# Local attention in a decoder on one core: score products of one head on half of the array's rows, softmax over eight heads at a time

## The chip, the cores and the metric

The kernel runs on one core of one Trainium2 chip. The metric is the device time of one execution in microseconds (us). A core has TensorE (PE, which multiplies matrices, and PEld, its loading of the stationary operand), VectorE (DVE), ScalarE (ACT), GpSimd (POOL) and the queues that issue DMAs (SP among them). Each runs its own list of instructions in order; semaphores tie the lists together. TensorE's results go to PSUM, eight banks of 512 fp32 numbers for each of 128 partitions; DVE and ACT read them from there.

## The reference, cut to what matters

A decoder of two blocks (a bidirectional Mamba layer, cross attention, a mixture of experts; then local attention, cross attention, another mixture of experts) on 32 sequences of 128 tokens of width 128, all in fp32. The change touches the local attention alone:

```python
H, KV, HD, WIN = 16, 4, 64, 64            # 16 query heads share 4 key/value heads
q = rmsnorm((x @ wq.T).reshape(B, T, H, HD), q_norm_w)
k = rmsnorm((x @ wk.T).reshape(B, T, KV, HD), k_norm_w)
v = (x @ wv.T).reshape(B, T, KV, HD)      # k and v repeated 4 times, to 16 heads
scores = einsum('bqhd,bkhd->bhqk', q, k) / sqrt(HD)
mask = (i >= j) & (i - j < WIN)
attn = softmax(where(mask, scores, -inf))
y = einsum('bhqk,bkhd->bqhd', attn, v).reshape(B, T, H * HD) @ wo.T
```

## The kernel before, in words

`program` (L2534) runs the six layers one after the other. `window_attention_layer` (L1790) walks the 32 sequences; each sequence has four slots q = 0 to 3, one for each quad of four heads that share a key/value head. All engines walk the same slots (`walk_sequences`, L203), each with its own `slot` function, and the order within a slot is the order of the code. In the slot (b, q) an engine works for several sequences at once: b itself, b + 1 (scores and softmax), b + 2 (transposes of q and k), b + 3 (the projection to q, k and v) and b - 1 (the output).

PE, in the order of its slot (L1877):

- `turn` (L1842): four transposes of the normalized probabilities of quad q of b into the PSUM tile `pt`; waits for POOL's `norm_ready`.
- `scores` of quad q of b + 1 (L1852): a product of the identity with the mask `outside` (bf16, 512 columns) sets the bank, then two fp32 products add the scores of two heads each: the stationary operand is a pair of heads of q (two times 64 rows), the moving one `kT`, which holds the transposed keys twice on the diagonal and zeros beside them, so that a product over 128 rows gives two heads. The two tiles `ps` are one bank each and take turns, so that quad q + 1 can be written while quad q is read.
- In slot 1: a transpose of the normalized input of b + 3, and twelve transposes of q and k of b + 2. In slot 2: the projection to q, k and v of b + 3 (L1897, L1899), then the output projection of b - 1 (L1920).
- `values` of the quad before (L1865): probabilities times values, two heads in each half of the columns.

The trace shows two instructions for each fp32 product, and one for each transpose or bf16 product.

DVE, in slot q: the row sum `den` (L2012) of the quad that comes up for division, the row maximum `top` (L2018) of a quad of fresh scores, the reciprocal of the first (L2025), the subtraction of the second (L2031). Behind these in slot 0: `xh` (L2041), then `qn` and `kn` (L2058, L2061), which wait for r, the reciprocal root of the mean squares of b + 2. In slot 2: a copy of v. In slot 3: the sum of squares (L2047) and the mean square (L2051) of b + 3, and the residual sum.

ACT: the copy of `py` to `cT`, exp (L1949) in place on `pr` two slots after the scores, the copy of the transposed probabilities (L1955), in slot 1 the copies to `qT` and `kT` (L1968, L1973: two instructions of 64 partitions for `kT`), in slot 2 the squares (L1980, L1983).

POOL, in slot q: the division `norm` (L2094), a product of `pr` with the reciprocals; in slot 3, behind the division of quad 0 of the next sequence, the power that gives r (L2104). The division of quad 1 in slot 0 stands behind it.

Of the kernel before, what the change touches and what calls it, by code (L numbers as in the profile page):

```python
# [37 lines left out]
QH = 4  # L38
# [1741 lines left out]
def window_weights(nc, ctx, w):  # L1780
    W = Weights(nc, ctx, "dw_")
    W.wq = W.tile("wq", [128, HL * HDL], w["wq"])
    W.wkv = W.tile("wkv", [128, 2 * KVL * HDL], w["wkv"])
    W.wo = W.tile("wo", [128, HL // 2, D], w["wo"])
    W.outside32 = W.tile("outside32", [128, T], w["outside"])
    W.qnw, W.knw = W.tile("qnw", [128, 1], w["qnw"]), W.tile("knw", [128, 1], w["knw"])
    return W


def window_attention_layer(nc, S, W, ahead):  # L1790
# [12 lines left out]
    with ExitStack() as ctx:  # L1803
        A = Alloc(nc, ctx, "d_")
        outside = A.sb("outside", [128, T], BF16)
        kscale = A.sb("kscale", [128, 1])
# [8 lines left out]
        qT = [A.sb(f"qT{p}", [128, NP, T]) for p in range(2)]  # L1815
        kT = [A.sb(f"kT{p}", [128, KVL, 2, T]) for p in range(2)]
        top, den, rden = ([A.sb(f"{n}{q}", [128, QH]) for q in range(NQ)] for n in ("top", "den", "rden"))
        pr = [A.sb(f"pr{q}", [128, QH, T]) for q in range(NQ)]
        prT = [A.sb(f"prT{q}", [128, QH, T]) for q in range(2)]
        cT = [A.sb(f"cT{p}", [128, NP, T]) for p in range(2)]  # L1820
        ps = [A.ps(f"ps{k}", [128, QH, T]) for k in range(2)]
        pt = A.ps("pt", [128, QH, T])
# [5 lines left out]
            ms_ready r_ready qn_ready kn_ready ve_ready v_ready qkT_mm qT_ready kT_ready s_mm top_ready sub_ready  # L1828
            exp_ready den_ready rden_ready norm_ready pt_mm prT_ready y_mm cT_ready o_mm x_ready stats kT_zero""".split()}
        with nc.Block() as block:  # L1830
# [6 lines left out]
            def _(pe):  # L1837
# [4 lines left out]
                def turn(b, q):  # L1842

                    t = b.quad(q)
                    pe.wait_ge(s["norm_ready"], t + 1)
                    if due(t):
                        pe.wait_ge(s["prT_ready"], t)
                    for i in range(QH):
                        ins = tr(pt[:, i, :], pr[q][:, i, :], S.ident[:, :])
                    ins.then_inc(s["pt_mm"], 1)  # L1850

                def scores(b, q):  # L1852
                    t = b.quad(q)
                    if q == 0:
                        pe.wait_ge(s["qT_ready"], 2 * (b.n + 1))
                        pe.wait_ge(s["kT_ready"], 2 * (b.n + 1))
                    if due(t - 1):
                        pe.wait_ge(s["sub_ready"], t - 1)
                    mm(ps[q % 2][:, :, :], S.ident_bf[:, :], bc(outside[:, :], 1, QH), start=True, stop=False)
                    for k in range(2):  # L1860
                        ins = mm(ps[q % 2][:, 2 * k:2 * k + 2, :], qT[b.p][:, 2 * q + k, :], kT[b.p][:, q, :, :],  # L1861
                                 start=False, stop=k == 1)
                    ins.then_inc(s["s_mm"], 1)

                def values(b, q):  # L1865
                    t = b.quad(q)
                    pe.wait_ge(s["prT_ready"], t + 1)
                    if q == 0:
                        pe.wait_ge(s["v_ready"], b.n + 1)
                    if due(t):  # L1870
                        pe.wait_ge(s["cT_ready"], t)
                    for k in range(2):
                        ins = mm(py[64 * k:64 * k + 64, 0:2 * T], v[b.p][:, q, :], prT[q % 2][:, k:QH:2, :],  # L1873
                                 start=True, stop=True)
                    ins.then_inc(s["y_mm"], 1)

                def slot(b, q):  # L1877
                    if b.real():
                        turn(b, q)
                    nxt = b.plus(1)  # L1880
                    if nxt.real():
                        scores(nxt, q)
                    n = b.plus(3)
# [6 lines left out]
                    if q == 2 and n.real():  # L1890
                        pe.wait_ge(s["xT_ready"], n.n + 1)
                        if due(2 * n.n):
                            pe.wait_ge(s["qT_ready"], 2 * n.n)
                        if due(2 * n.n):
                            pe.wait_ge(s["kT_ready"], 2 * n.n)
                        for k in range(2):
# [32 lines left out]
            def _(act):  # L1929
                A_ = nc.scalar.activation  # L1930
                act.wait_ge(s["kscale"], 2)
                act.wait_ge(s["kT_zero"], 2)

                def slot(b, q):
# [28 lines left out]
                    if q == 1 and m.real():  # L1963
                        if due(NQ * (m.n - 1)):
                            act.wait_ge(s["s_mm"], NQ * (m.n - 1))
# [5 lines left out]
                        for k in range(2):  # L1971
                            half = slice(64 * k, 64 * k + 64)
                            A_(kT[m.p][half, :, k, :], pkv[half, :].rearrange("p (i t) -> p i t", t=T), ACT.Copy,  # L1973
                               scale=kscale[half, 0:1]).then_inc(s["kT_ready"], 1)
                    if q == 2 and n.real():
# [18 lines left out]
            def _(dve):  # L1994
                V = nc.vector
                dve.wait_ge(W.loaded, W.all())
                for p in range(2):
                    V.memset(kT[p][:, :, :, :], 0.0).then_inc(s["kT_zero"], 1)
                V.tensor_copy(outside[:, :], W.outside32[:, :]).then_inc(s["prep"], 1)

# [5 lines left out]
                def slot(b, q):  # L2006
                    d = b if q < 3 else b.plus(1)
                    if d.real():
                        qd = (q + 1) % NQ
                        t = d.quad(qd)  # L2010
                        dve.wait_ge(s["exp_ready"], t + 1)
                        V.tensor_reduce(den[qd][:, :], pr[qd][:, :, :], AX.X, ALU.add).then_inc(s["den_ready"], 1)  # L2012
                    a = b if q < 1 else b.plus(1)
                    if a.real():
                        qa = (q + 3) % NQ
                        t = a.quad(qa)
                        dve.wait_ge(s["s_mm"], t + 1)
                        V.tensor_reduce(top[qa][:, :], ps[qa % 2][:, :, :], AX.X, ALU.max  # L2018
                                        ).then_inc(s["top_ready"], 1)
                    if d.real():  # L2020
                        t = d.quad(qd)
                        dve.wait_ge(s["den_ready"], t + 1)
                        if due(t - 3):
                            dve.wait_ge(s["norm_ready"], t - 3)
                        V.reciprocal(rden[qd][:, :], den[qd][:, :]).then_inc(s["rden_ready"], 1)  # L2025
                    if a.real():
                        t = a.quad(qa)
                        dve.wait_ge(s["top_ready"], t + 1)
                        if due(t - 3):
                            dve.wait_ge(s["pt_mm"], t - 3)  # L2030
                        V.tensor_tensor(pr[qa][:, :, :], ps[qa % 2][:, :, :], bc(top[qa][:, :], 2, T),  # L2031
                                        ALU.subtract).then_inc(s["sub_ready"], 1)
# [50 lines left out]
            def _(pool):  # L2083
# [4 lines left out]
                def slot(b, q):  # L2088
                    d = b if q < 3 else b.plus(1)
                    if d.real():  # L2090
                        qd = (q + 1) % NQ
                        t = d.quad(qd)
# [465 lines left out]
def layout(inputs):  # L2558
# [10 lines left out]
    for p in "fb":  # L2569
# [34 lines left out]
    a.update({"D_wq": f[n + "wq"].T, "D_wkv": np.concatenate([f[n + "wk"], f[n + "wv"]]).T,  # L2604
              "D_wo": f[n + "wo"].T.reshape(HL // 2, 128, D).transpose(1, 0, 2),
              "D_outside": np.where((i >= j) & (i - j < WIN), 0.0, MASKED).astype(np.float32),
              "D_qnw": np.tile(f[n + "q_norm_w"], 2)[:, None], "D_knw": np.tile(f[n + "k_norm_w"], 2)[:, None]})
# [33 lines left out]
```

## Time and profile before

| | |
|---|---|
| timed runs, median of 3 (lowest to highest) | 2488.03 us (2478.44 to 2491.33) |
| the profiled execution | 2469.95 us |
| its span, first to last instruction | 2468.2 us |
| mean granted clock of TensorE | 0.924 |
| busy over the span: PE, DVE, ACT, POOL | 84%, 76%, 58%, 57% |
| the local attention's first and last instruction, about | 1527 and 2045 us |

The page cuts the span into 40 slices of 61.7 us; the local attention fills slices 26 to 33. The timeline view lists instructions of an engine in order of time, neighbours of one kind merged; the duration that it gives for several is from the first start to the last end, so the time that they hold the engine is better read from start to start. In square brackets stands the idle time before an instruction and what ended it. Ends of PE's instructions are modelled and include the way through the array, so rows of PE overlap.

### The profile page before, as it was taken

Reading aid. Unit: us, or ns where it says so; the run is one execution under the profiler, and the core shown is the slowest. Engines: PE = TensorE matmul, PEld = TensorE weight load, DVE = VectorE, ACT = ScalarE, POOL = GpSimd, SP = SyncE. Lnnn points to the kernel's source line nnn. Section 1 sums busy time; section 2 is a strip of 40 time slices with the busy share of each in tenths; the row PEclk is TensorE's granted clock in tenths of the full one; section 3 lists DMA queues with packets and bytes.
Section 4 is the critical chain, followed back from the end, with each engine's and each line's share of the span. In section 5 each row is a group of like instructions: output and inputs, shape, how many; then the busy total and the mean of one; then the engine's idle time right before and its main releaser. Section 6 shows DMA issues by size and latency. Waiting matters only on the chain. (4 is left out here: it accounts for less than half of the span.)

```text
span 2468.2 us, 43398 instructions
## 1 busy us (share of the span) xinstructions
PE 2078.3 (84%) x13248; PEld 1323.3 (54%) x13248; DVE 1879.3 (76%) x3049; ACT 1431.6 (58%) x2678; POOL 1410.2 (57%) x1050
## 2 busy tenths in 40 slices
PE   3888888888888886899865892799999998998486
PEld 1333343334333333677643782466666666777476
DVE  5999999999999997677644334588888885777445
ACT  4667666667666662466542551466666664665254
POOL 4788788878788885333254454355545543332546
PEclk7999999999999999799986996899999998999588
DMA  4222222222222221200111222000000001000442
GB/s 122 74 76 74 74 73 74 73 73 73 73 73 72 76 75 45 74 12 12 31 39 58 82 80 79 1 1 0 0 0 0 0 1 57 12 12 13 140 143 72
DMA packets 104165, 130.67 MB, mean 53 GB/s; under 512 B 33412, under 2 KB 65462, under 8 KB 103376
## 3 DMA queue, kind: packets, MB, share of 16 engines
q1 hardware_dynamic: 95344, 111.19, 15.5%
q0 software_dynamic: 8192, 17.59, 2.0%
q8 instruction: 48, 0.79, 0.1%
q10 hardware_dynamic: 512, 0.53, 0.1%
q14 instruction: 69, 0.57, 0.1%
HBM read 111.16 MB, written 25.20 MB: 55 GB/s over the span
## 5 line engine op out<-in xcount | busy, mean ns | idle before, releaser
L858 POOL TENSOR_TENSOR m_hc<-m_h,m_cs 128x1024 f32<-128x1024 f32 x256 | 602.8, 2359 | 179.8 <-DVE m_h L768 165.5
L768 DVE TENSOR_TENSOR_SCAN m_h<-m_da,m_pdb 128x1024 f32<-128x1024 f32 x256 | 585.1, 2286 | 28.3 <-DVE m_pdb L740 3.9
L461 PE MATMUL m_py<-m_hc,ident 128*128 128x512 f32 x1024 | 505.2, 617 | 1.9 <-POOL m_hc L858 1.9
L643 ACT ACTIVATE m_da<-m_dt,m_aneg 128x508 f32<-128x508 f32 x512 | 331.8, 709 | 115.9 <-DVE m_h L768 103.3
L740 DVE TENSOR_TENSOR m_pdb<-m_du,m_pdb 128x1024 f32<-128x1024 f32 x256 | 309.0, 1207 | 22.8 <-PE m_pdb L448 13.7
L461 PEld LDWEIGHTS m_py<-m_hc,ident 128*128 128x128 f32 x1024 | 199.4, 197 | 220.6 <-issue 211.3
L2094 POOL TENSOR_TENSOR d_pr<-d_pr,d_rden 128x512 f32<-128x512 f32 x128 | 133.0, 1039 | 177.2 <-DVE d_rden L2025 177.2
L1111 ACT ACTIVATE x_prT<-x_pt 77x512 f32<-77x512 f32 x256 | 137.8, 586 | 132.9 <-PE x_pt L1013 132.0
L1227 POOL TENSOR_TENSOR x_kd<-x_kT,x_hm 128x308 f32<-128x308 f32 x64 | 45.1, 704 | 273.8 <-ACT x_v_raw L1123 273.8
L448 PE MATMUL m_pdb<-m_bcrow,m_sel 96*128 96x512 bf16 x256 | 100.3, 392 | 112.2 <-DVE m_h L768 112.2
L2104 POOL TENSOR_TENSOR d_r<-d_mean_sq,minus_half 128x20 f32<-128x20 f32 x32 | 113.1, 3534 | 75.8 <-DVE d_mean_sq L2051 75.8
L448 PEld LDWEIGHTS m_pdb<-m_bcrow,m_sel 96*128 96x128 bf16 x256 | 25.5, 100 | 228.7 <-DVE m_h L768 183.8
L1013 PE MATMUL x_pt<-ident,x_pr 128*77 128x128 f32 x1024 | 140.3, 281 | 0.2
L1013 PEld LDWEIGHTS x_pt<-ident,x_pr 128*77 128x77 f32 x1024 | 118.4, 151 | 28.1 <-issue 24.0
L1861 PE MATMUL d_ps<-d_kT,d_qT 128*128 128x256 f32 x512 | 132.9, 382 | 0.0
L407 PE MATMUL m_pm<-m_xnT,m_wtap 128*128 128x512 f32 x256 | 124.7, 611 | 1.3 <-ACT m_xnT L558 1.3
L1173 DVE TENSOR_REDUCE x_top<-x_ps 128x8 f32<-128x616 f32 x128 | 101.8, 796 | 28.5 <-PE x_ps L1035 11.3
L1775 POOL DMA_INDIRECT c_routed<-c_done,c_to x80 | 78.6, 983 | 71.1 <-DVE c_done L1738 47.2
L1159 DVE RECIPROCAL x_rden<-x_pyo 128x128 f32<-128x128 f32 x64 | 61.3, 957 | 70.4 <-PE x_pyo L1067 70.4
L1179 DVE TENSOR_TENSOR x_pr<-x_ps,x_top 128x616 f32<-128x616 f32 x128 | 102.3, 800 | 14.1
L1943 ACT ACTIVATE d_cT<-d_py 128x256 f32<-128x256 f32 x128 | 49.1, 384 | 108.6 <-PE d_py L1873 107.8
L2012 DVE TENSOR_REDUCE d_den<-d_pr 128x4 f32<-128x512 f32 x128 | 87.1, 681 | 29.7 <-ACT d_pr L1949 29.2
(315 smaller groups left out, 4638.0 us busy)
## 6 DMA issues: line engine op xcount, KB each, us to landing
m_cs<-crow SPq DMA_DIRECT2D x256, 256.0 KB, 3.0
f_row<-f_sorted SPq DMA_DIRECT2D x24, 400.0 KB
c_row<-c_sorted SPq DMA_DIRECT2D x40, 144.0 KB
c_back_in<-c_routed SPq DMA_DIRECT2D x16, 256.0 KB, 3.3
f_sorted<-in_F_blank SPq DMA_DIRECT2D x9, 400.0 KB
cw_gud<-in_C_gud SPq DMA_DIRECT2D x1, 3456.0 KB
x<-in_x SPq DMA_DIRECT2D x8, 256.0 KB, 4.3
fw_w<-in_F_w SPq DMA_DIRECT2D x1, 2048.0 KB, 8.6
```

Source lines behind the costliest of these rows:

```text
L407: ins = mm(pm[1 - c][:, :], wtap[:, d, k, c * 128:(c + 1) * 128], xnT[:, par[0], :, off:off + T], start=k == 0, stop=k == TAPS - 1)
L448: mm(pdb[:, row_bank(n), :], sel[:, n, :], bcrow[d][:, :], start=True, stop=True).then_inc(s["b_mm"], 1)
L461: ins = mm(py[:, c, :], S.ident[:, :], hc[n % BUF][:, c, :], start=False, stop=n == NS - 1)
L643: A_(dst, src, ACT.Exp, scale=aneg[:, d, c, n:n + 1]).then_inc(s["da_ready"], 1)
L740: V.tensor_tensor(out, du[d][:, ::-1, :], bc(pdb[:, row_bank(n), :], 1, CH), ALU.mult).then_inc(s["db_ready"], 1)
L768: V.tensor_tensor_scan(h[n % BUF][:, way], da[n % BUF][:, d:d + CH * GT][:, way], pdb[:, b:b + 2, :].rearrange("p c t -> p (c t)")[:, way] ...
L858: P.tensor_tensor(hc[n % BUF][:, :, :], h[n % BUF][:, :].rearrange("p (c t) -> p c t", c=CH), bc(cs[n % BUF][:, :], 1, CH), ALU.mult).then ...
L1013: ins = tr(pt[e][0:TC, i * T:(i + 1) * T], pr[u.p][u.h][:, QH * e + i, :], S.ident[:, :])
L1111: A_(prT[u.p][Q2 * u.h + e][:, :], pt[e][0:TC, :], ACT.Copy).then_inc(s["prT_ready"], 1)
L1861: ins = mm(ps[q % 2][:, 2 * k:2 * k + 2, :], qT[b.p][:, 2 * q + k, :], kT[b.p][:, q, :, :], start=False, stop=k == 1)
L2094: P.tensor_tensor(pr[qd][:, :, :], pr[qd][:, :, :], bc(rden[qd][:, :], 2, T), ALU.mult).then_inc(s["norm_ready"], 1)
L2104: P.tensor_tensor(r[:, :], mean_sq[:, :], S.minus_half[:, 0:NH], ALU.pow).then_inc(s["r_ready"], 1)
```

## The change

Scores are computed for eight heads at a time, a pair of quads e = 0 or 1, in slots 0 and 2. `ps` becomes one tile of two banks: even heads in the first, odd heads in the second. Each head is a product of its own over 64 rows: q of an even head lies on partitions 0 to 63, q of an odd head on 64 to 127, and `kT` holds the same transposed keys on both halves, with no zeros (its two memsets go, and one ACT copy of 128 partitions takes the place of two). The mask is set by four products instead of one for a bank: the first over 128 rows with the first 64 columns of the identity, the other three of 64 rows by 64 columns. DVE does den, top, reciprocal and subtract on eight heads (128 x 1024) in slots 1 and 3, and nothing of the softmax in slots 0 and 2; ACT's exp takes eight heads in slots 0 and 2. POOL's division, `turn` and `values` stay with four heads in each slot; a quad is now four heads of one parity, and `wo` is laid out in the new order of heads on the host. The core of the diff:

```diff
-        ps = [A.ps(f"ps{k}", [128, QH, T]) for k in range(2)]
+        ps = A.ps("ps", [128, 2 * QH, T])
...
-                    if due(t - 1):
-                        pe.wait_ge(s["sub_ready"], t - 1)
-                    mm(ps[q % 2][:, :, :], S.ident_bf[:, :], bc(outside[:, :], 1, QH), start=True, stop=False)
-                    for k in range(2):
-                        ins = mm(ps[q % 2][:, 2 * k:2 * k + 2, :], qT[b.p][:, 2 * q + k, :], kT[b.p][:, q, :, :],
-                                 start=False, stop=k == 1)
+                    if due(pair(b, e)):
+                        pe.wait_ge(s["sub_ready"], pair(b, e))
+                    mm(ps[0:64, of(0), :], S.ident_bf[:, 0:64], bc(outside[:, 0, :], 1, QH), start=True, stop=False)
+                    for rows, h in ((0, 1), (1, 0), (1, 1)):
+                        half, to = slice(64 * h, 64 * h + 64), slice(64 * rows, 64 * rows + 64)
+                        mm(ps[to, of(h), :], S.ident_bf[half, half], bc(outside[half, rows, :], 1, QH),
+                           start=True, stop=False)
+                    for i in range(QH):
+                        kv = 2 * e + i // 2
+                        for h in range(2):
+                            half = slice(64 * h, 64 * h + 64)
+                            ins = mm(ps[:, QH * h + i, :], qT[b.p][half, 2 * kv + i % 2, :], kT[b.p][half, kv, :],
+                                     start=False, stop=i == QH - 1)
...
-                    if nxt.real():
-                        scores(nxt, q)
+                    if nxt.real() and q % 2 == 0:
+                        scores(nxt, q // 2)
...
-                    if e.real():
-                        qe = (q + 2) % NQ
-                        act.wait_ge(s["sub_ready"], e.quad(qe) + 1)
-                        A_(pr[qe][:, :, :], pr[qe][:, :, :], ACT.Exp).then_inc(s["exp_ready"], 1)
+                    if e.real() and q % 2 == 0:
+                        half = (q + 2) % NQ // 2
+                        p = pr[2 * e.p + half]
+                        act.wait_ge(s["sub_ready"], pair(e, half) + 1)
+                        A_(p[:, :, :], p[:, :, :], ACT.Exp).then_inc(s["exp_ready"], 1)
...
+                    d, a = (b, b.plus(1)) if q < 3 else (b.plus(1), b.plus(1))
+                    ed, ea = (1, 0) if q < 3 else (0, 1)
+                    kd, ka = 2 * d.p + ed, 2 * a.p + ea
+                    if q % 2 and d.real():
+                        dve.wait_ge(s["exp_ready"], pair(d, ed) + 1)
+                        V.tensor_reduce(den[kd][:, :], pr[kd][:, :, :], AX.X, ALU.add).then_inc(s["den_ready"], 1)
+                    if q % 2 and a.real():
+                        dve.wait_ge(s["s_mm"], pair(a, ea) + 1)
+                        V.tensor_reduce(top[ka][:, :], ps[:, :, :], AX.X, ALU.max).then_inc(s["top_ready"], 1)
+                    if q % 2 and d.real():
+                        dve.wait_ge(s["den_ready"], pair(d, ed) + 1)
...
+                        V.reciprocal(rden[kd][:, :], den[kd][:, :]).then_inc(s["rden_ready"], 1)
+                    if q % 2 and a.real():
...
+                        V.tensor_tensor(pr[ka][:, :, :], ps[:, :, :], bc(top[ka][:, :], 2, T),
                                         ALU.subtract).then_inc(s["sub_ready"], 1)
...
-                        pool.wait_ge(s["rden_ready"], t + 1)
-                        P.tensor_tensor(pr[qd][:, :, :], pr[qd][:, :, :], bc(rden[qd][:, :], 2, T), ALU.mult
+                        k, h = 2 * d.p + qd // 2, qd % 2
+                        pool.wait_ge(s["rden_ready"], pair(d, qd // 2) + 1)
+                        P.tensor_tensor(pr[k][:, of(h), :], pr[k][:, of(h), :], bc(rden[k][:, of(h)], 2, T), ALU.mult
```

## Rows read from the trace of the kernel before

**Rows 1.** Windows, the steady stretch: us, busy (instructions), PEclk, DMA share, GB/s.
```profile
core 0: us, PE busy (x) PEld busy (x) DVE busy (x) ACT busy (x) POOL busy (x), PEclk, DMA share, GB/s
1585.13:2003.28 418.15, 413.67 (x2422) 287.54 (x2421) 362.76 (x698) 283.32 (x589) 214.29 (x140) 1.00 0.00 0
```

**Rows 2.** Groups by line, 1585 to 2003: count | busy, mean ns | idle before.
```profile
L2104 POOL TENSOR_TENSOR d_r<-d_mean_sq,minus_half 128x20 f32<-128x20 f32 x28 | 98.9, 3533 | 57.9 <-DVE d_mean_sq L2051 57.9
```

**Rows 3.** Timeline of POOL: start, us, engine, line, operation, tiles, [idle before <-releaser].
```profile
1799.17 3.53 POOL L2104 TENSOR_TENSOR d_r<-d_mean_sq,minus_half 128x20 f32<-128x20 f32 x1 [2.11 <-DVE d_mean_sq L2051]
1802.67 1.04 POOL L2094 TENSOR_TENSOR d_pr<-d_pr,d_rden 128x512 f32<-128x512 f32 x1
1806.07 1.04 POOL L2094 TENSOR_TENSOR d_pr<-d_pr,d_rden 128x512 f32<-128x512 f32 x1 [2.36 <-DVE d_rden L2025]
...
1814.12 3.53 POOL L2104 TENSOR_TENSOR d_r<-d_mean_sq,minus_half 128x20 f32<-128x20 f32 x1 [2.04 <-DVE d_mean_sq L2051]
```

**Rows 4.** Timeline of PE, slots 0 to 2 of one sequence.
```profile
1802.05 1.03 PE L1861 MATMUL d_ps<-d_kT,d_qT 128*128 128x256 f32 x4
1803.00 0.65 PE L1873 MATMUL d_py<-d_prT,d_v 128*64 128x256 f32 x4
1803.77 0.66 PE L1849 MATMUL d_pt<-ident,d_pr 128*128 128x128 f32 x4
1804.26 0.38 PE L1859 MATMUL d_ps<-d_outside,ident_bf 128*128 128x512 bf16 x1
1804.47 1.03 PE L1861 MATMUL d_ps<-d_kT,d_qT 128*128 128x256 f32 x4
1805.34 0.27 PE L1889 MATMUL d_px<-ident,d_xh 128*128 128x128 f32 x1
...
1807.43 0.65 PE L1849 MATMUL d_pt<-ident,d_pr 128*128 128x128 f32 x4
...
1809.00 1.88 PE L1897 MATMUL d_pq<-dw_wq,d_xT 128*128 128x512 f32 x4
...
1811.58 1.95 PE L1920 MATMUL d_px<-dw_wo,d_cT 128*128 128x128 f32 x16
```

**Rows 5.** Timeline of DVE, slots 0 and 1 of the same sequence, and its sum of squares.
```profile
1802.83 1.29 DVE L2058 TENSOR_TENSOR d_qn<-d_pq,d_r 128x512 f32<-128x512 f32 x2 [0.30 <-POOL d_r L2104]
1804.04 0.68 DVE L2061 TENSOR_TENSOR d_kn<-d_pkv,d_r 128x512 f32<-128x512 f32 x1
1804.64 0.67 DVE L2012 TENSOR_REDUCE d_den<-d_pr 128x4 f32<-128x512 f32 x1
...
1805.83 0.16 DVE L2025 RECIPROCAL d_rden<-d_den 128x4 f32<-128x4 f32 x1
1806.03 0.69 DVE L2031 TENSOR_TENSOR d_pr<-d_ps,d_top 128x512 f32<-128x512 f32 x1
...
1812.19 1.49 DVE L2047 TENSOR_REDUCE d_ssq<-d_sq 128x20 f32<-128x1280 f32 x1 [0.51 <-ACT d_sq L1983]
```

**Rows 6.** The page's costliest groups: a 1024-wide DVE operation of the Mamba layer.
```profile
L740 DVE TENSOR_TENSOR m_pdb<-m_du,m_pdb 128x1024 f32<-128x1024 f32 x256 | 309.0, 1207 | 22.8 <-PE m_pdb L448 13.7
```

**Rows 7.** Timeline of PE in cross attention: column groups of 32, row groups of 32.
```profile
1103.21 1.08 PE L1063 MATMUL x_pyo<-x_prT,x_va 77*32 77x128 f32 x32
1104.11 1.06 PE L1067 MATMUL x_pyo<-x_prT,x_unit 77*32 77x128 f32 x32
1105.09 0.79 PE L1028 MATMUL x_ps<-x_kd,x_qT 32*128 32x308 f32 x4
1105.72 0.30 PE L1035 MATMUL x_ps<-x_out_of,x_fill 32*128 32x308 bf16 x2
```

**Rows 8.** Timeline of DVE at the start of the local attention.
```profile
1531.75 0.40 DVE L2041 TENSOR_SCALAR d_xh<-x,mean,rstd 128x128 f32<-128x128 f32 x1 [2.16 <-POOL rstd L136]
```

**Rows 9.** Windows in the first mixture of experts, columns as in rows 1.
```profile
1466.00:1470.00 4.00, 1.96 (x14) 1.67 (x13) 0.78 (x3) 1.45 (x4) 1.33 (x3) 1.00 0.25 70
1470.00:1473.38 3.38, 3.38 (x10) 2.67 (x10) 1.28 (x4) 1.94 (x5) 2.77 (x3) 0.50 0.32 94
...
1390.00:1394.00 4.00, 2.49 (x16) 2.36 (x17) 2.38 (x8) 2.83 (x6) 0.98 (x1) 1.00 0.07 13
```

More of the change, by code:

```diff
@@ L1784, in window_weights @@
     W.wo = W.tile("wo", [128, HL // 2, D], w["wo"])
-    W.outside32 = W.tile("outside32", [128, T], w["outside"])
+    W.outside32 = W.alloc.sb("outside32", [128, 2, T])
+    for half in range(2):
+        W.part(W.outside32[64 * half:64 * half + 64, :, :], w["outside"])
     W.qnw, W.knw = W.tile("qnw", [128, 1], w["qnw"]), W.tile("knw", [128, 1], w["knw"])
@@ L1815, in window_attention_layer @@
         qT = [A.sb(f"qT{p}", [128, NP, T]) for p in range(2)]
-        kT = [A.sb(f"kT{p}", [128, KVL, 2, T]) for p in range(2)]
-        top, den, rden = ([A.sb(f"{n}{q}", [128, QH]) for q in range(NQ)] for n in ("top", "den", "rden"))
-        pr = [A.sb(f"pr{q}", [128, QH, T]) for q in range(NQ)]
+        kT = [A.sb(f"kT{p}", [128, KVL, T]) for p in range(2)]
+        top, den, rden = ([A.sb(f"{n}{k}", [128, 2 * QH]) for k in range(4)] for n in ("top", "den", "rden"))
+        pr = [A.sb(f"pr{k}", [128, 2 * QH, T]) for k in range(4)]
         prT = [A.sb(f"prT{q}", [128, QH, T]) for q in range(2)]
         cT = [A.sb(f"cT{p}", [128, NP, T]) for p in range(2)]
-        ps = [A.ps(f"ps{k}", [128, QH, T]) for k in range(2)]
+        ps = A.ps("ps", [128, 2 * QH, T])
         pt = A.ps("pt", [128, QH, T])
@@ L1828, in window_attention_layer, with pair, of @@
             ms_ready r_ready qn_ready kn_ready ve_ready v_ready qkT_mm qT_ready kT_ready s_mm top_ready sub_ready
-            exp_ready den_ready rden_ready norm_ready pt_mm prT_ready y_mm cT_ready o_mm x_ready stats kT_zero""".split()}
+            exp_ready den_ready rden_ready norm_ready pt_mm prT_ready y_mm cT_ready o_mm x_ready stats""".split()}
+        def pair(b, e):
+            return 2 * b.n + e
+        def of(h):
+            return slice(QH * h, QH * h + QH)
         with nc.Block() as block:
@@ L1848, in turn, with scores @@
                     for i in range(QH):
-                        ins = tr(pt[:, i, :], pr[q][:, i, :], S.ident[:, :])
+                        ins = tr(pt[:, i, :], pr[2 * b.p + q // 2][:, QH * (q % 2) + i, :], S.ident[:, :])
                     ins.then_inc(s["pt_mm"], 1)
-                def scores(b, q):
-                    t = b.quad(q)
-                    if q == 0:
+                def scores(b, e):
+                    if e == 0:
                         pe.wait_ge(s["qT_ready"], 2 * (b.n + 1))
-                        pe.wait_ge(s["kT_ready"], 2 * (b.n + 1))
-                    if due(t - 1):
-                        pe.wait_ge(s["sub_ready"], t - 1)
-                    mm(ps[q % 2][:, :, :], S.ident_bf[:, :], bc(outside[:, :], 1, QH), start=True, stop=False)
-                    for k in range(2):
-                        ins = mm(ps[q % 2][:, 2 * k:2 * k + 2, :], qT[b.p][:, 2 * q + k, :], kT[b.p][:, q, :, :],
-                                 start=False, stop=k == 1)
+                        pe.wait_ge(s["kT_ready"], b.n + 1)
+                    if due(pair(b, e)):
[11 more added lines that the diff above has]
+                                     start=False, stop=i == QH - 1)
                     ins.then_inc(s["s_mm"], 1)
@@ L1872, in values @@
                     for k in range(2):
-                        ins = mm(py[64 * k:64 * k + 64, 0:2 * T], v[b.p][:, q, :], prT[q % 2][:, k:QH:2, :],
-                                 start=True, stop=True)
+                        ins = mm(py[64 * k:64 * k + 64, 0:2 * T], v[b.p][:, 2 * (q // 2) + k, :],
+                                 prT[q % 2][:, 2 * k:2 * k + 2, :], start=True, stop=True)
                     ins.then_inc(s["y_mm"], 1)
@@ L1893, in slot @@
                             pe.wait_ge(s["qT_ready"], 2 * n.n)
-                        if due(2 * n.n):
-                            pe.wait_ge(s["kT_ready"], 2 * n.n)
+                        if due(n.n):
+                            pe.wait_ge(s["kT_ready"], n.n)
                         for k in range(2):
@@ L1963, in slot @@
                     if q == 1 and m.real():
-                        if due(NQ * (m.n - 1)):
-                            act.wait_ge(s["s_mm"], NQ * (m.n - 1))
+                        if due(2 * (m.n - 1)):
+                            act.wait_ge(s["s_mm"], 2 * (m.n - 1))
                         for k in range(2):
@@ L1970, in slot @@
                         act.wait_ge(s["qkT_mm"], 3 * m.n + 3)
[L1971 to L1974, printed above, removed]
+                        A_(kT[m.p][:, :, :], pkv[:, :].rearrange("p (i t) -> p i t", t=T), ACT.Copy,
+                           scale=kscale[:, 0:1]).then_inc(s["kT_ready"], 1)
                     if q == 2 and n.real():
@@ L1996, in _ @@
                 dve.wait_ge(W.loaded, W.all())
-                for p in range(2):
-                    V.memset(kT[p][:, :, :, :], 0.0).then_inc(s["kT_zero"], 1)
-                V.tensor_copy(outside[:, :], W.outside32[:, :]).then_inc(s["prep"], 1)
+                V.tensor_copy(outside[:, :, :], W.outside32[:, :, :]).then_inc(s["prep"], 1)
                 V.tensor_tensor(kscale[:, :], W.qnw[:, :], W.knw[:, :], ALU.mult).then_inc(s["kscale"], 1)
@@ L2006, in slot @@
                 def slot(b, q):
[L2007 to L2031, printed above, removed]
+                    d, a = (b, b.plus(1)) if q < 3 else (b.plus(1), b.plus(1))
@@ new lines, in slot @@
+                    if q % 2 and d.real():
+                        dve.wait_ge(s["den_ready"], pair(d, ed) + 1)
+                        if due(2 * (pair(d, ed) - 3)):
+                            dve.wait_ge(s["norm_ready"], 2 * (pair(d, ed) - 3))
+                        V.reciprocal(rden[kd][:, :], den[kd][:, :]).then_inc(s["rden_ready"], 1)
+                    if q % 2 and a.real():
+                        dve.wait_ge(s["top_ready"], pair(a, ea) + 1)
+                        if due(2 * (pair(a, ea) - 3)):
+                            dve.wait_ge(s["pt_mm"], 2 * (pair(a, ea) - 3))
+                        V.tensor_tensor(pr[ka][:, :, :], ps[:, :, :], bc(top[ka][:, :], 2, T),
@@ L2604, in layout @@
     a.update({"D_wq": f[n + "wq"].T, "D_wkv": np.concatenate([f[n + "wk"], f[n + "wv"]]).T,
-              "D_wo": f[n + "wo"].T.reshape(HL // 2, 128, D).transpose(1, 0, 2),
-              "D_outside": np.where((i >= j) & (i - j < WIN), 0.0, MASKED).astype(np.float32),
+              "D_wo": f[n + "wo"].T.reshape(2, 2, 2, 2, HDL, D).transpose(1, 4, 0, 3, 2, 5).reshape(128, HL // 2, D),
+              "D_outside": np.where((i >= j) & (i - j < WIN), 0.0, MASKED).astype(np.float32
+                                    ).reshape(2, 64, T).transpose(1, 0, 2),
               "D_qnw": np.tile(f[n + "q_norm_w"], 2)[:, None], "D_knw": np.tile(f[n + "k_norm_w"], 2)[:, None]})
```

4 lines of the change are left out of this document (1 added, 3 removed).

## The prediction

> **What bounds the kernel now.** The page puts the local attention in slices of full clock with PE and DVE both busy, so I read its steady stretch by windows, then each engine in order of time over one sequence, looking for what closes the cycle. From the fourth q/k/v projection to the last, 28 sequences take 418.15 us, 14.93 each, at clock 1.00, PE busy 99%, DVE 87% [rows 1, 2]. PE looks like the bound, but its busy time hides waits at both ends of a cycle that goes through all engines. It runs so (times from the timelines):
> - POOL ends r, the power for a later sequence, at 1799.17 + 3.53 = 1802.70, and only then does norm 1 (1802.67 to 1803.71) [rows 3]; PE's turn 1 starts at 1803.77 [rows 4], just as norm 1 lands.
> - From turn 1, PE needs 3.66 us to turn 2 (1807.43), 1.57 more to the q/k/v projection (1809.00), 2.58 for that (to 1811.58, where the output projection starts) [rows 4].
> - The squares, their sum, the mean square and the next r end at 1814.12 + 3.53 = 1817.65 [rows 3]: 6.07 us after 1811.58.
>
> So 1.07 + 3.66 + 1.57 + 2.58 + 6.07 = 14.95, the period between the two r. Call this loop A, and the end of r "R". A second loop, B, starts at R too, through DVE: it waits for r, makes qn (1802.83) and kn (1804.04), then the first softmax work of slot 1: den 1804.64, then top, reciprocal 1805.83, and POOL's norm 2 runs 1806.07 to 1807.11 [rows 3, 5], 0.32 us before PE comes to turn 2. Loop B has 0.3 us of slack; any lengthening of it beyond that is paid in every sequence.
>
> **The change, part by part.**
>
> *DVE's order.* Each 512-wide den, top and subtract becomes half of a 1024-wide one. From den to reciprocal, two 512-wide ones take 1.19 us, 0.60 each [rows 5], and 512 more elements cost 1.207 - 0.69 = 0.52 by a 1024-wide operation elsewhere (1207 ns) [rows 6] against the 0.69 of a 512-wide one. So 1.12 each: per sequence 2 x 3 x (1.20 - 1.12) = 0.5 us less, and two reciprocals fewer: some 0.8 us of busy time. But DVE isn't full, so the sum doesn't count; the place does. All softmax work leaves slots 0 and 2 and gathers in 1 and 3. In slot 0, DVE now has only xh, then the wait for r, qn and kn. The den of the second half, which norm 2 needs, stands behind them, as before, but it is now twice as long, and so is the top between it and the reciprocal. Worked out from R: qn at R + 0.13, kn at R + 1.34, den at R + 1.94 (as now) [rows 3, 5]; top at R + 3.06; reciprocal at R + 4.18; norm 2 starts 0.24 after that (1805.83 to 1806.07) at R + 4.42 and ends at R + 5.46; turn 2 starts at R + 5.52, against 1807.43 - 1802.70 = R + 4.73 now. The exp for this den stands in ACT's slot 0, behind a copy that follows the last values of slot 3, so it ends about 1 us before R and is no part of the loop.
>
> *PE's scores.* Four calls of 1.08 us (1804.26 to 1805.34) [rows 4] become two of a length S. In slot 2, between turn 2 and the projection, a pair of 1.08 becomes S for eight heads; slots 1 and 3 lose theirs. S is not in the trace. Its parts by rows: a change of array shape costs 0.95 - 0.87 = 0.08 us (four score products followed by values, of 64 columns, from 1802.05; by a product of the same shape, from 1804.47) [rows 4]. Mask: a bf16 piece of 512 columns takes 0.21 (1804.26 to 1804.47) [rows 4]; the first has 128 rows and 64 columns and runs alone, the other three are 64 by 64. I take these three as beside each other, so twice 0.21 + 0.08, 0.58 in all; in turn they would add 0.42. Heads: 16 instructions (the trace has two for each fp32 product) on alternating row halves. Cross attention shows two row groups beside each other: four instructions of 308 columns from 1105.09 to 1105.72, 0.63 [rows 7], where one after the other at the rate of the 256-wide ones (0.87 for four) they would be 1.05. It also shows 32 products of 128 columns in four column groups, 8 turns, in 0.90 [rows 7]. So 8 turns, 0.90, with 0.11 to fill. And 0.08 to change back. S = 0.58 + 1.01 + 0.08, about 1.7. Ends: all four mask pieces beside each other and no price for shapes, 0.21 + 0.90 = 1.1; nothing beside anything, 4 x 0.29 + 16 x 0.12 (that is, 1.95 / 16 of a pass with its own weights, the output projection [rows 4]) = 3.1. I take 1.7, because row groups and column groups both stand side by side in these rows; with the three mask pieces in turn it would be 2.1.
>
> For the three pieces of 64 by 64 the Trainium skill has a rule that no row here shows: "TensorEngine Tiling (Array Packing)", Key Properties, says that tiles run independently, and in the same list that a change of the tiling mode drains the engine. By it the three pieces run together and S stays at 1.7; were it not to hold for this mix, a sequence would be 0.4 us longer.
>
> *One PSUM tile for the scores.* Scores of the second half now wait for the subtract of the first, which was a bank away. That subtract starts 0.20 after the reciprocal [rows 5], at R + 4.38, and ends 1.2 later, at R + 5.6; PE comes to the scores at R + 5.52 + 0.49 = R + 6.01. Hidden by 0.4 us; scores of the first half, in slot 0, have some 4 us. Behind this wait stand the projection and all of loop B, so each tenth beyond 0.4 would be paid.
>
> *ACT.* Two 64-row copies into kT become one, and two exp one of 1024. ACT has a third of its time free [rows 1] and the exp that loop B needs is early by some 3 us (R - 1 against den at R + 1.94), so nothing. The exp of slot 2 now waits for the later subtract and is longer, and den in slot 3 waits for it; that work ends at about R + 10.3, still ahead of the last square that the sum of squares waits for (R + 11).
>
> *POOL, values, output.* Same counts and sizes; order of heads only: 0.
>
> *Start and end.* The two memsets of kT go and one more small DMA comes; DVE waited 2.16 us there for POOL's first power anyway [rows 8]: 0. The four sequences without a projection lose r from their loop; PE's saving of 2 x (2.16 - 1.7) counts there, three or four times, against DVE's longer chain: -3 to +3, taken as 0.
>
> *The sum.* Loop B: turn 2 at R + 5.52, 0.49 for the turn (1803.77 to 1804.26 [rows 4]), S, 2.58 for the projection, 6.07 to the next R: 14.66 + S = 16.36. Loop A: 1.07 + (3.66 - 1.08) + 0.49 + S + 2.58 + 6.07 = 12.79 + S = 14.49, so it falls out of the bound. PE and DVE have less work than either. So 16.36 - 14.93 = 1.43 us per sequence, 28 times: 40 us. The profiled execution, 2469.95 us (span 2468.2), would be 2510. The timed runs lie above it (median 2488.03), so I add to these: 2528. With the ends of S, +0.84 to +2.83 per sequence: 2512 to 2567.
>
> **Rivals.**
>
> *Clock lost (slower still).* PE would now stand idle some 1.9 us before turn 2 in each sequence. The trace shows both outcomes of such a gap: PE was busy 1.96 of 4 us at 1466 to 1470 and the granted clock was 0.50 (1.2 GHz) right behind, to 1473.38; it was busy 2.49 of 4 at 1390 to 1394 and the clock stayed at 1.00 [rows 9]. If the fall comes every time, and lasts as long as in that row (3.38 us) on scores and projection, it costs up to 1.7 us: 28 x 1.7 = 47 more, 2575. For it: scores and projection follow the gap at once. Against: PE is dense on both sides of it. If it falls one time in four, 12 us.
>
> *The pairs don't pair (slower still).* S = 3.1, 2567. Against it, rows 7.
>
> *Loop B doesn't close (not slower).* If den and reciprocal of the second half came to run while DVE waits for r, norm 2 would follow norm 1 and end at R + 2.1, and loop A would bind: 14.49, 28 x 0.44 = 12 us faster, 2476; with S = 1.1, 29 us faster, with S = 2.1 no change. It decides where norm 2 lands before PE is through with slot 1, 1.07 + 2.58 after R, that is before R + 3.65. For it: DVE has more time free than before. Against: engines take their instructions in order, and the code puts den behind kn, and top between den and reciprocal.
>
> **How the numbers follow.** About 0.5%, 12 us, is what a measurement of this kernel tells from no change. Forecast 0.70, clock lost in most sequences 0.10, pairs that don't pair 0.06, loop B not closed 0.14, of which half faster by over 0.5% and the rest within it. So faster 0.07, same 0.08 (with the low end of loop B), slower 0.85. Range for 8 in 10: below, the low end of S (2512) and some 15 us for start, end and the spread of the runs, 2497; above, clock lost at every gap with a few us to spare, 2580.
>
> **What would show it.** Right: r every 16.4 us; DVE idle about 3 us for r ahead of qn, with no softmax work in slot 0; den (1.2 us) right behind kn; PE idle 1.5 to 2 us before turn 2 and released by POOL's norm; scores of eight heads in 1.7 us with pairs of starts a few ns apart; clock 1.00 in most of the stage. Wrong: turn 2 right behind values without a wait, a period under 15 us (loop A), starts of score products 0.1 us apart throughout (no pairs), a wait of scores for the subtract, or a clock well under 1.00.

## The result, and the profile after

The changed kernel takes 2532.69 us (median of four runs; before, 2485.24 in the same comparison): 47.4 us more, ratio 1.0191, 95% interval 1.0152 to 1.0231. One of the four, of 4119 us, was disturbed and is left out of the ratio; the other three (2527.34, 2529.63, 2535.75) have their median at 2529.63, 44.4 us above the kernel before. The forecast was 2528, slower.

The same 28 sequences as in [rows 1], in windows:

```profile
1598.07:2063.92 465.85, 408.63 (x2982) 258.96 (x2980) 356.43 (x474) 256.64 (x504) 213.38 (x140) 1.00 0.00 0
```

465.85 against 418.15 us is 47.7 more, 16.64 a sequence instead of 14.93: all of the difference of the timed runs, 44 to 47 us. PE's busy share falls from 99% to 88%, DVE's from 87% to 77%. The mean granted clock rounds to 1.00 in both; after the change it fell once, in the first of these sequences (see "Clock lost" below). PE, DVE and ACT are busy for less time than before, POOL for the same, and all wait longer. The spans of the two profiled executions differ by 65.8 us, but 13.7 of that lies ahead of the local attention, in code that is the same in both: its first projection starts at 1533.19 before and at 1546.86 after. From there to the start of its last output projection (2042.52 and 2105.46) the traces differ by 49.3 us.

POOL after, one period, to be held against [rows 3]:

```profile
1802.78 3.53 POOL L2110 TENSOR_TENSOR d_r<-d_mean_sq,minus_half 128x20 f32<-128x20 f32 x1 [2.66 <-DVE d_mean_sq L2057]
1806.28 1.04 POOL L2100 TENSOR_TENSOR d_pr<-d_pr,d_rden 128x512 f32<-128x512 f32 x1
1810.78 2.04 POOL L2100 TENSOR_TENSOR d_pr<-d_pr,d_rden 128x512 f32<-128x512 f32 x2 [3.46 <-DVE d_rden L2032]
...
1819.43 3.53 POOL L2110 TENSOR_TENSOR d_r<-d_mean_sq,minus_half 128x20 f32<-128x20 f32 x1 [2.65 <-DVE d_mean_sq L2057]
```

R, the end of r, is 1806.31, and the next r ends at 1822.96, 16.65 later. DVE between (against [rows 5]):

```profile
1803.35 0.35 DVE L2047 TENSOR_SCALAR d_xh<-x,mean,rstd 128x128 f32 x1
1806.44 1.29 DVE L2064 TENSOR_TENSOR d_qn<-d_pq,d_r 128x512 f32<-128x512 f32 x2 [2.74 <-POOL d_r L2110]
1807.65 0.68 DVE L2067 TENSOR_TENSOR d_kn<-d_pkv,d_r 128x512 f32<-128x512 f32 x1
1808.25 1.21 DVE L2024 TENSOR_REDUCE d_den<-d_pr 128x8 f32<-128x1024 f32 x1
1809.37 1.22 DVE L2027 TENSOR_REDUCE d_top<-d_ps 128x8 f32<-128x1024 f32 x1
1810.50 0.20 DVE L2032 RECIPROCAL d_rden<-d_den 128x8 f32<-128x8 f32 x1
1810.73 1.23 DVE L2037 TENSOR_TENSOR d_pr<-d_ps,d_top 128x1024 f32<-128x1024 f32 x1
```

DVE stands idle for 2.74 us until r lands, and only then come qn, kn and two wide steps; the reciprocal that division 2 needs starts at R + 4.19, where before it was at 1805.83, R + 3.13. Then PE (against [rows 4]):

```profile
1807.38 0.66 PE L1859 MATMUL d_pt<-ident,d_pr 128*128 128x128 f32 x4 [0.27 <-POOL d_pr L2100]
1807.87 0.27 PE L1905 MATMUL d_px<-ident,d_xh 128*128 128x128 f32 x1
1808.44 1.06 PE L1924 MATMUL d_pq<-ident,d_qn 128*128 128x128 f32 x8 [0.30 <-issue]
...
1809.87 0.65 PE L1889 MATMUL d_py<-d_prT,d_v 128*64 128x256 f32 x4
1811.87 0.65 PE L1859 MATMUL d_pt<-ident,d_pr 128*128 128x128 f32 x4 [1.35 <-POOL d_pr L2100]
1812.46 0.40 PE L1868 MATMUL d_ps<-d_outside,ident_bf 128*64 128x512 bf16 x1
1812.79 0.41 PE L1871 MATMUL d_ps<-d_outside,ident_bf 64*64 64x512 bf16 x3
1813.13 1.16 PE L1877 MATMUL d_ps<-d_kT,d_qT 64*128 64x128 f32 x16
1814.22 1.98 PE L1913 MATMUL d_pq<-dw_wq,d_xT 128*128 128x512 f32 x4
...
1816.90 1.95 PE L1936 MATMUL d_px<-dw_wo,d_cT 128*128 128x128 f32 x16
```

Turn 2 now waits 1.35 us for POOL, and everything from there to the next r moves with it. Sixteen head instructions take 1.09 us and three mask pieces 0.34: the new products do run beside each other.

### The profile page after: what moved, and what is told of

Read it like the earlier page. It is cut to its first block and busy times, and to the rows that moved or that the text cites. A ratio compares the mean times of both kernels' runs of the same rounds, so it can differ in the third digit from the quotient of the medians.

```text
span 2534.0 us, 44119 instructions
## 1 busy us (share of the span) xinstructions
PE 2072.1 (82%) x13888; PEld 1292.3 (51%) x13888; DVE 1867.4 (74%) x2791; ACT 1402.2 (55%) x2582; POOL 1408.6 (56%) x1050
## 3 DMA queue, kind: packets, MB, share of 16 engines
q1 hardware_dynamic: 95360, 111.26, 14.9%
## 5 line engine op out<-in xcount | busy, mean ns | idle before, releaser
L1859 PE MATMUL d_pt<-ident,d_pr 128*128 128x128 f32 x512 | 83.8, 287 | 58.8 <-POOL d_pr L2100 53.6
L1859 PEld LDWEIGHTS d_pt<-ident,d_pr 128*128 128x128 f32 x512 | 54.0, 141 | 113.8 <-POOL d_pr L2100 84.5
L1028 PE MATMUL x_ps<-x_kd,x_qT 32*128 32x308 f32 x512 | 106.7, 494 | 4.4 <-issue 3.4
```

The costliest lines, as they stand in the source:

```text
L1859: ins = tr(pt[:, i, :], pr[2 * b.p + q // 2][:, QH * (q % 2) + i, :], S.ident[:, :])
```

## The experiments

Each was run beside the kernel before on one chip. "Period" is the mean distance from one r to the next in the steady stretch of its trace; where two kernels' totals lie within the spread of their runs, the period decides. The diffs from here on name the steps in their order instead of the whole code.

**Reciprocal ahead of top.** In DVE's slot:

```diff
-  den; top; reciprocal; subtract
+  den; reciprocal; top; subtract
```

> The changed kernel with one step of DVE turned round: in slots 1 and 3 the reciprocal comes right behind den, ahead of top. Its period in the trace is 16.65 us. Theory (loop B through DVE's den, top, reciprocal and POOL's norm 2 sets the period; one PSUM tile is the next limit right behind it): norm 2 comes 1.0 us earlier, but the subtract that frees the tile stays where it was (it ends 0.45 us before the scores need it now), so the scores wait for it and the period falls only by 0.3 to 0.45, to about 16.3: some 10 us faster than the changed kernel. Rival (the PSUM tile costs nothing): the whole 1.0 less, 15.6, 29 us faster. Rival (the longer scores on PE are the loss, DVE's order is not): no change, 16.65.

Measured: 2527.13 us, ratio 1.0182 (1.0165 to 1.0199); period 16.50. DVE and PE:

```profile
1798.73 1.21 DVE L2024 TENSOR_REDUCE d_den<-d_pr 128x8 f32<-128x1024 f32 x1
1799.97 0.20 DVE L2029 RECIPROCAL d_rden<-d_den 128x8 f32<-128x8 f32 x1
1800.09 1.22 DVE L2032 TENSOR_REDUCE d_top<-d_ps 128x8 f32<-128x1024 f32 x1
1801.45 1.23 DVE L2037 TENSOR_TENSOR d_pr<-d_ps,d_top 128x1024 f32<-128x1024 f32 x1
```

```profile
1801.35 0.65 PE L1859 MATMUL d_pt<-ident,d_pr 128*128 128x128 f32 x4 [0.35 <-POOL d_pr L2100]
1802.73 0.40 PE L1868 MATMUL d_ps<-d_outside,ident_bf 128*64 128x512 bf16 x1 [0.73 <-DVE d_pr L2037]
```

Turn 2's wait falls from 1.35 to 0.35 (0.46 in every other sequence), and the scores behind it wait 0.73 for the subtract. The period fell by 0.15, less than the 0.3 to 0.45 that I expected: the reciprocal right behind den starts 0.12 us later than top did (1.24 after den for 1.12) and holds DVE for another 0.12, where before it fitted into the 1.36 us from top to subtract for nothing; so the subtract itself starts at R + 4.65 instead of R + 4.42. The rival that gives 15.6 is out. Against 16.65 the period moved by only 0.15; what speaks against that rival here is the 1.0 us that turn 2's wait lost, and the next experiment decides it. The one score tile is a second limit right behind loop B.

**Softmax of the second half ahead of r.** ACT makes its exp at the head of slot 3, DVE its den and reciprocal at the head of slot 0:

```diff
 ACT, slot 3:  + exp(b + 1, second half), ahead of cT          slot 0:  - exp(b, second half)
 DVE, slot 0:  + den, reciprocal (b, second half), ahead of xh  slot 1:  - den, reciprocal
```

> The changed kernel with the softmax of the second half taken out of the way of r: ACT makes its exp at the head of slot 3, DVE its den and reciprocal at the head of slot 0, ahead of xh and of the wait for r (DVE is idle there for 2.74 us). Same instructions, same sizes. Theory (loop B): norm 2 is ready right after norm 1, turn 2 no longer waits (PE comes to it at R + 4.14), and the period is 4.14 + 0.49 + 1.86 + 2.68 + 6.06 = 15.2: 40 us faster than the changed kernel, about 2493, level with the kernel before within 10 us. Rival (PE's new scores are the loss): no change, 16.65. Rival (loop A as the prediction had it, 12.79 + 1.86): 14.65, 10 us faster than the kernel before.

Measured: 2488.63 us, ratio 1.0031 (1.0013 to 1.0050); period 15.24, as expected by loop B. In DVE's timeline the wait for r is down to 1.09 us, since den and reciprocal stand in it; PE goes from values to turn 2 without a wait. Two r (POOL), then DVE, then PE:

```profile
1785.29 3.53 POOL L2116 TENSOR_TENSOR d_r<-d_mean_sq,minus_half 128x20 f32<-128x20 f32 x1 [2.44 <-DVE d_mean_sq L2063]
...
1800.52 3.53 POOL L2116 TENSOR_TENSOR d_r<-d_mean_sq,minus_half 128x20 f32<-128x20 f32 x1 [2.37 <-DVE d_mean_sq L2063]
```

```profile
1801.09 1.22 DVE L2030 TENSOR_REDUCE d_den<-d_pr 128x8 f32<-128x1024 f32 x1
1802.44 0.20 DVE L2038 RECIPROCAL d_rden<-d_den 128x8 f32<-128x8 f32 x1
1802.73 0.35 DVE L2053 TENSOR_SCALAR d_xh<-x,mean,rstd 128x128 f32 x1
1804.18 1.29 DVE L2070 TENSOR_TENSOR d_qn<-d_pq,d_r 128x512 f32<-128x512 f32 x2 [1.09 <-POOL d_r L2116]
```

```profile
1790.94 1.06 PE L1924 MATMUL d_pq<-ident,d_qn 128*128 128x128 f32 x8 [0.29 <-issue]
...
1792.37 0.65 PE L1889 MATMUL d_py<-d_prT,d_v 128*64 128x256 f32 x4
1792.95 0.66 PE L1859 MATMUL d_pt<-ident,d_pr 128*128 128x128 f32 x4
```

The same instructions in another place give back 1.41 of the 1.72 us that each sequence lost. That is the cause shown. It also shows what the prediction's loop A left out: turn 2 comes at R + 4.13, not R + 3.65, because the transposes of q and k stand 0.3 to 0.5 us for qn and kn, which the scores of slot 1 used to cover. (The split wait below takes that wait away, and there turn 2 does come at R + 3.65.)

**Heads by half, unpaired.**

```diff
-  for i in range(QH): for h in range(2): product(h, i)
+  for h in range(2): for i in range(QH): product(h, i)
```

> The changed kernel with the eight head products of a pair ordered by half: four even heads, then four odd ones, so that neighbours stand on the same 64 rows and can't run beside each other. Theory (alternating halves pair up; scores of slot 2 lie in loop B): 16 starts about 0.11 apart, 1.8 us instead of 1.09, period 17.3 to 17.4, some 20 us slower than the changed kernel. Rival (TensorE finds the pairs by itself from further back, or scores are hidden): 16.65.

One run, 2565.92 us; period 17.2.

```profile
1804.06 1.71 PE L1877 MATMUL d_ps<-d_kT,d_qT 64*128 64x128 f32 x16
1805.70 0.65 PE L1889 MATMUL d_py<-d_prT,d_v 128*64 128x256 f32 x4
```

1.64 us instead of 1.09, 0.55 more, and the period is 0.55 longer: the scores of slot 2 are in the loop, one to one. I expected 1.8; the first five starts are 0.11 to 0.21 apart, and the sixth falls 6 ns behind the fifth, which I read as the first odd head beside the fifth even instruction (the trace doesn't name the half).

In two of the 28 sequences of this trace the period is 18.8 instead of 17.2. In both, the granted clock fell to 0.50 (1.2 GHz) in the heads and the projection, right behind the usual wait of 1.36 us before turn 2. One of them:

```profile
1810.57 0.66 PE L1859 MATMUL d_pt<-ident,d_pr 128*128 128x128 f32 x4 [1.36 <-POOL d_pr L2100]
...
1811.82 2.48 PE L1877 MATMUL d_ps<-d_kT,d_qT 64*128 64x128 f32 x16
1814.23 2.83 PE L1913 MATMUL d_pq<-dw_wq,d_xT 128*128 128x512 f32 x4
```

```profile
1813.00:1816.00 3.00, 3.00 (x11) 1.84 (x8) 1.64 (x3) 0.00 (x0) 0.24 (x1) 0.50 0.00 0
```

That is the prediction's "clock lost", at 1.6 us a fall where it gave up to 1.7. The total of this one run thus holds more than the order of the heads.

**Mask by one product for each bank.**

```diff
-  four pieces: 128 rows x 64 columns, then three of 64 x 64
+  for h in range(2): mm(ps[:, of(h), :], ident_bf[:, :], bc(outside[:, :], 1, QH), start=True, stop=False)
```

> The changed kernel with the mask set by one product of 128 rows and 128 columns for each bank, instead of four pieces in two array shapes. Theory (each change of shape costs about 0.1 us and the four pieces take two turns of 0.33): two turns of 0.215, one change of shape less, scores 0.2 us shorter, period 16.4 to 16.5, 6 us faster than the changed kernel (seen in the trace, too little for the total). Rival (the small pieces are what makes the mask cheap): slower than 16.65.

One run, 2525.47 us; period 16.41, 0.24 less.

```profile
1804.83 0.66 PE L1857 MATMUL d_pt<-ident,d_pr 128*128 128x128 f32 x4 [1.36 <-POOL d_pr L2095]
1805.32 0.59 PE L1867 MATMUL d_ps<-d_outside,ident_bf 128*128 128x512 bf16 x2
1805.85 1.16 PE L1872 MATMUL d_ps<-d_kT,d_qT 64*128 64x128 f32 x16
1806.94 1.98 PE L1908 MATMUL d_pq<-dw_wq,d_xT 128*128 128x512 f32 x4
```

From turn 2 to the projection, 2.11 us instead of 2.35. Wait and heads are as they were (1.36 and 1.09). The total of one run decides nothing here; the period does.

**Split wait for qn and kn**, on top of the second experiment:

```diff
-  wait qn (both halves), kn, v_early; 8 transposes of q; 4 of k
+  wait first half of qn; 4 transposes; wait second half; 4; wait kn, v_early; 4 of k
```

> The run with den and exp of the second half moved forward (period 15.24 in its trace) and one more step: PE waits for each half of qn and for kn apart, instead of for all of them ahead of the first transpose. In that trace PE waits 0.3 to 0.5 us for kn at the head of slot 1. Theory (the loop now runs R, qn, kn, transposes, values, turn 2; the PSUM tile is the next limit, its subtract ending at R + 4.3): turn 2 would come 0.46 us earlier, but the scores behind it then wait some 0.2 us for the subtract: period 14.9, level with the kernel before, about 9 us less than without this step. Rival (the tile is free): 14.77. Rival (PE's own work is the bound by now): no change, 15.24.

Measured: 2481.31 us, ratio 0.9990 (0.9973 to 1.0007); period 15.08 where I expected 14.9. Turn 2 comes at R + 3.65, 0.48 earlier, and the wait has moved on to the score tile; the subtract that frees it ends at R + 4.50, not at R + 4.3:

```profile
1804.74 0.66 PE L1859 MATMUL d_pt<-ident,d_pr 128*128 128x128 f32 x4
1805.65 0.40 PE L1868 MATMUL d_ps<-d_outside,ident_bf 128*64 128x512 bf16 x1 [0.26 <-DVE d_pr L2043]
```

**The same, with the mask of one product and division 1 ahead of r.**

```diff
 POOL:  - slot 3: division 0, r;  slot 0: 1;  slot 1: 2;  slot 2: 3
        + slot 3: divisions 0 and 1, r;  slot 0: 2;  slot 1: 3
```

> As the run with the split wait, and two steps more: the mask set by one 128 x 128 product for each bank (0.23 us a pair less in its own run), and POOL divides quad 1 ahead of r, quad 2 right behind r. Theory: turn 1 no longer waits for r, the scores are 1.64 us, and what is left is R, qn, kn, top, subtract (R + 4.35), scores, projection: 4.37 + 1.64 + 2.68 + 6.06 = 14.75 with the PSUM tile's wait as the bound; about 2476, 5 to 6 us under the kernel before. Rival (POOL's order is the bound, loop A): below 14.5. Rival (PE's sum): 13.9.

Measured: 2478.03 us, ratio 0.9977 (0.9963 to 0.9991); period 14.94 where I expected 14.75.

```profile
1800.69 0.65 PE L1857 MATMUL d_pt<-ident,d_pr 128*128 128x128 f32 x4
1802.01 0.61 PE L1867 MATMUL d_ps<-d_outside,ident_bf 128*128 128x512 bf16 x2 [0.67 <-DVE d_pr L2038]
```

The score tile is the bound, as named; the subtract that frees it ends at R + 4.50 rather than 4.35, because the subtract still starts 1.35 us after top, though no reciprocal stands between, and I had given it 1.2. Shortening PE ahead of it gains nothing as long as that wait stands: 0.67 us.

**Projection ahead of the scores.** In slot 2 PE projects first, and DVE sums the squares ahead of top:

```diff
 PE, slot 2:   - turn, scores, projection, output   + turn, projection, scores, output
 DVE, slot 3:  - den, top, reciprocal, subtract, squares   + den, reciprocal, squares, top, subtract
```

> The changed kernel (exp in its place) with the order made round r: PE in slot 2 does the projection ahead of the scores; DVE does the reciprocal right behind den, and in slot 3 the sum of squares ahead of top and subtract; POOL divides quad 1 ahead of r; PE's split wait and the 128 x 128 mask as in the run before. Theory (what cost the time is what stands between two r; with scores, top and subtract of the second half out of that stretch, r comes early and TensorE's own work of about 13.9 us is the bound): period 13.9 to 14.2, PE gapless, 21 to 29 us under the kernel before, about 2456. Rival (the one PSUM tile with its chain of scores, top, subtract twice a sequence bounds): 14.7 or more. Rival (the wide DVE steps late in slot 3 delay qn of the next sequence): 14.4.

Measured: 2461.69 us, ratio 0.9902 (0.9881 to 0.9923); period 14.44 (14.41 and 14.47 by turns). Windows, then PE:

```profile
1700.00:1900.00 200.00, 192.19 (x1424) 125.94 (x1420) 169.54 (x235) 120.18 (x249) 105.48 (x70) 1.00 0.00 0
```

```profile
1790.45 0.66 PE L1857 MATMUL d_pt<-ident,d_pr 128*128 128x128 f32 x4 [0.49 <-POOL d_pr L2099]
1790.94 1.88 PE L1908 MATMUL d_pq<-dw_wq,d_xT 128*128 128x512 f32 x4
...
1793.52 0.59 PE L1867 MATMUL d_ps<-d_outside,ident_bf 128*128 128x512 bf16 x2
```

PE is busy 96%, and the score tile has left the loop (the scores follow the projection at once). Turn 2 still waits 0.4 to 0.5 us for division 2, so 13.9 was not reached. The third guess named 14.4, but not for this reason: DVE stands idle 0.2 to 0.4 us ahead of qn, waiting for r, so its wide steps don't hold qn up; den and reciprocal still stand behind qn and kn, as in loop B. This version beats both kernels. It has six steps at once, and which of them gives how much wasn't taken apart.

**That order with the old products.** The kernel before, with projection first, reciprocal behind den, squares ahead of top, split wait. POOL's order stays as it was (division 1 behind r):

> The kernel before, with its own score products, its two score tiles and its softmax over four heads, but with the order of the best run so far: projection ahead of the scores in slot 2, reciprocal right behind den, the sum of squares ahead of top in slot 3, and the split wait for qn and kn. It tells how much of that run's 0.990 is the order and how much the new products. Theory (the new products save TensorE 2 x 0.45 us a sequence, which counts only where the order lets TensorE be the bound): here TensorE's own 14.6 us bound, period 14.6 to 14.7 against 14.94, 7 to 10 us faster than the kernel before. Rival (the order is all of it): 14.4 or less, as in that run. Rival (division 1 behind r still bounds): 14.9.

Measured: 2494.44 us, ratio 1.0059 (1.0032 to 1.0086); period 15.53. All three guesses miss.

```profile
1795.79 0.65 PE L1849 MATMUL d_pt<-ident,d_pr 128*128 128x128 f32 x4
1796.99 1.96 PE L1897 MATMUL d_pq<-dw_wq,d_xT 128*128 128x512 f32 x4 [0.55 <-ACT d_kT L1975]
```

With the scores out of the way, the projection comes to the PSUM banks before ACT has copied kT, and turn 2 to projection takes 1.20 us where the turn needs 0.50: 0.70 lost. I see no other wait on PE in these rows, so its own work is about 15.53 - 0.70 = 14.8, not 14.6. The kernel before, at 14.93, already stood within 0.2 us of that: with the old products no order can gain more, and the 14.44 of the run before needs the new ones. The change's single copy of kT would probably take away most of the 0.70, since the wait is for the second of ACT's two copies; that wasn't run.

## Why the prediction was right

| us | before | forecast | after |
|---|---|---|---|
| R to turn 2 | 4.73 | 5.52 | 5.56 |
| turn 2 to projection | 1.57 | 2.19 | 2.35 |
| projection | 2.58 | 2.58 | 2.68 |
| its end to the next R | 6.07 | 6.07 | 6.06 |
| period | 14.95 | 16.36 | 16.65 |

(Before, R to turn 2 is PE's own way there, loop A; forecast and after, it is DVE's and POOL's, loop B.) The mechanism is the one forecast, and its main term was right; the terms that were off are these.

- *DVE's order* was right to 0.04 us: den at R + 1.94, top R + 3.06, reciprocal R + 4.19, turn 2 at R + 5.56. The experiment that moves den and reciprocal shows that this place, not a sum of work, makes the loss.
- *PE's scores*: S was 1.86 (1812.36, the end of the turn's 0.49, to 1814.22) for 1.7. The heads are as worked out: 1.09 with the change back, for 1.01 + 0.08. The mask is 0.77 for 0.58: a change of shape costs 0.10 to 0.12, not 0.08, and the sum counted two of them up to the heads where there are three (it left out the one from 64 by 64 to the heads' shape). The projection is also 0.10 longer behind the other shape, which the sum had at nothing. Together 0.26 a sequence, or 7 us. That is about what the forecast of 40 us more lacked against the 47.4. That the totals lie only 5 apart is luck: the kernel before took 2485.24 here and 2488.03 in the runs that the forecast started from.
- On the three pieces of 64 by 64, the Trainium skill states in "TensorEngine Tiling (Array Packing)", Key Properties, that tiles run independently and that a change of the tiling mode drains the engine. The first half agrees with this trace: the three are 0.41 us from the first start to the last end, where the piece of 128 by 64 before them is 0.40. Of the second half the trace shows a price for each change, 0.10 to 0.12 us, but not that it is a drain.
- *DVE's busy time* fell by 0.23 us a sequence (362.76 to 356.43 over 28), not by the 0.8 given; the copy of v (L2076, before L2070) alone takes 0.41 more, 1.04 in the mean for 0.63. As the prediction said, this sum doesn't count.
- *One score tile*: hidden, with 0.50 us from the subtract's end (1811.96) to the mask's start (1812.46), for the 0.4 given. The first, fifth and sixth experiments show it as the next limit.
- *Start and end* taken as 0: in the traces 1.6 us, 49.3 from the first projection to the last output projection against 47.7 in the steady stretch. The timed runs can't tell that from 0.
- *Clock lost*: happened once in the 28 sequences, and cost nothing there. In the first, PE stood 1.93 us for division 1, and the granted clock was 0.50 behind it; but division 2, which starts at 1611.07 and takes 1.04 us, ended only just ahead of turn 2 (1612.16), and that sequence took 16.44 us, less than the mean (projection at 1598.07 to projection at 1614.51).

```profile
1607.77 0.96 PE L1859 MATMUL d_pt<-ident,d_pr 128*128 128x128 f32 x4 [1.93 <-POOL d_pr L2100]
```

```profile
1608.00:1611.00 3.00, 3.00 (x16) 2.84 (x15) 3.00 (x6) 1.66 (x4) 0.00 (x0) 0.50 0.00 0
```

  In the others PE stood idle 0.27, 0.30 and 1.35 us by its rows, and the clock stayed at 1.00. The gap before turn 2 was 1.35 and not the 1.9 forecast, because the transposes wait for qn and kn ahead of it, which the prediction left out. So the gap that the rival spoke of didn't come about. It was no idle worry: the unpaired run, with 1.36, lost the clock twice, at 1.6 us each.
- *Pairs that don't pair*: refuted, 1.09 against 1.64 us in the unpaired run.
- *Loop B doesn't close*: it closed. The rival's own sum was wrong, though: with den out of the way the period is 15.24, slower than before, not 14.49. It lacked the wait for qn and kn (0.48) and 0.26 of scores and projection. With the wait alone, 14.97, it would have been no faster than the kernel before.

## What to carry to other kernels

Before batching steps of an engine that is not the bound, find the loop that sets the period and ask where the batched step falls in it: here DVE was busy 6 us less over 28 sequences and each sequence grew 1.7, most of it because two steps twice as long stood behind a wait for another engine. Work that is ready ahead of such a wait belongs ahead of it. And after each gain name the next limit: here norm, the wait for qn and kn, and the score tile stood behind one another, and each step after the first gained only 0.1 to 0.5 us a sequence before the next one held.

## What the runs showed of the hardware

- Products on alternating 64-row halves ran two at a time: their instructions start in pairs a few ns apart, 0.11 us from pair to pair (fp32, 128 columns, weights loaded for each), 16 in 1.09 us. Grouped by half they still overlapped where the halves meet: 16 instructions in 1.64 us rather than 1.8.
- Each change of array shape cost TensorE 0.10 to 0.12 us, so a mask in four small pieces (0.77) was dearer than two full products of 512 columns and one change (0.53). The first instructions behind a change were about 0.1 us slower again (the projection 2.68 for 2.58).
- DVE's copy of v took 0.28 us where POOL stood idle beside it (the first and the projection-first experiment). In the changed kernel it took 1.04 in the mean; in the sequence above it starts while POOL divides and ends 0.14 us behind POOL (1811.87 + 1.09 against 1810.78 + 2.04).
- A granted clock of 0.50 followed a wait of PE of 1.93 us in the changed kernel, and two of the 28 waits of 1.36 us in the unpaired run; it followed none of the later waits of 1.35 us in the changed kernel.
